# A delta-rule attention layer with a mixture of experts: later scatter waits, small scalings on ScalarE, padding a group ahead, a three-engine final sum

## The chip, the cores and the metric

The kernel runs on one core of one Trainium2 chip. The time is that of one execution on the device, in microseconds (us); a run gives one such time. The engines are TensorE (PE, its weight loads PEld), VectorE (DVE), ScalarE (ACT), GpSimd (POOL) and SyncE (SP, which here only issues DMAs). A q behind an engine's name (SPq, DVEq) is its instruction queue. Numbers such as L1143 are lines of the kernel before; the changed kernel's lines lie some 10 to 50 further down.

## The reference

The input is 2 x 2048 tokens of 128 features in float32. Two blocks follow, each on the layer-normed input and added to it.

```
x = x + attention(layernorm(x))
x = x + experts(layernorm(x))
```

The attention is a gated delta rule with 8 heads of 128 x 128 state. Projections give q, k and v, each run through a causal convolution of four taps; two more give the gates beta and alpha.

```
S = S * alpha_t ;  kv = k_t S ;  S = S + outer(k_t, (v_t - kv) * beta_t) ;  o_t = q_t S      (token by token)
out = (o / rms(o) * norm_w * silu(z)) @ out_w.T
```

The experts: a router picks the best 2 of 8 experts for each token, with softmax weights over these two; each expert computes `relu(x W1 + b1) W2 + b2` with 512 hidden features, and the two results are summed with their weights.

## The kernel before

**Chunks and groups.** The delta rule is computed in chunks of 128 tokens. With decays, key products and the inverse of a triangular matrix a chunk becomes matrix products, and only the state S goes from chunk to chunk. A group is two chunks (c = 0, 1), sixteen groups in all, and the eight heads are worked on in two halves (u = 0, 1). `stages(g, a, par)` finishes group g while it prepares group a = g + 1, on each engine in the same order, which is the long string `ORDER` (L248): a word such as `scale.0` is the step `scale` for chunk 0. Each engine walks through `ORDER` and issues what is its own; all else is done by semaphores. Groups 1 to 14 run in a hardware loop of two groups a turn (L643 for GpSimd, and the same on the others), so every second group begins with a turn of the loop. An engine executes its instructions in order: a wait holds everything behind it.

**Steps of a group that matter here.** `taps`, `first` and `last` are the convolution of one of sixteen weight tiles: ScalarE multiplies two taps (L749), VectorE adds two (L1111, L1114), GpSimd adds the halves (L625). `diag` (L617, GpSimd) and `scan` (L1122, VectorE) build the decays; `ka` and `aq` (L608) scale keys and queries by them, `sp` (L637) scales the state. `kk` is the product of the keys (TensorE), `nm` masks it. `scale` (L1143, L1144, VectorE) takes the decays of the chunk's end, 128 x 8 elements, for ScalarE's `kd` (L758) and for GpSimd's `sp`. `inv` are 22 parts of the triangular inversion on VectorE (L1006 to L1028). `sq` (L808, ScalarE) sums squares of the output, and `rms` (L1046 to L1056, with L229 to L236) is a chain of small VectorE steps to one over the root; `gn` (L817) scales by it, `gt` transposes, `out` projects, `x2` (L1190) adds the residual, which SP has loaded (`xl`, L483) and stores again (`xs`, L489).

**Routing.** Each finished group g is routed during the next one (`route`): `sm` and `s2` its layer norm on ScalarE, `nr` the normalised rows on GpSimd (L581, L584), `xt`, `lg` the router's logits, `rk` the ranks (L1057), `pf` and `ps` the places in the experts' regions (L1085), and `sc` four indirect DMAs on GpSimd (L597) that scatter the rows into the DRAM tensor `rows_in`, at the place that is next in their expert's region. `sw` at the end of `ORDER` (L588) waits for these four scatters before GpSimd's next group. `counts` holds where each expert's rows end.

**Between the two blocks.** The last group is routed after the loop. Then VectorE makes ready the experts' second bias `b2` as two float16 rows (L1229, L1230), copies the ends of the regions (L1235) and works out the table of the 39 tiles of 256 rows (L1236 to L1264): expert, first row, limit. SP writes 256 rows of zeros behind each expert's last row (L520 to L523, nine DMAs), so that a tile never reads rows that weren't written, and then gathers the tiles (L532). VectorE goes on with the first bias for all tiles (L1268, L1270) and the softmax weights of the two experts of each token (L1276 to L1285, with one exponential on ScalarE, L848).

**The expert tiles.** For tile t: gather, transpose (L1630), split into a high and a low float16 half (L853, L1295), `up` (twelve products, L1643), bias and relu (L860 and L1302), split again (L867, L1310), `down` (L1649: two products of one row each with `b2`, high and low, L1657, and twelve with W2 in each half), scaling (L1315), and two indirect DMAs that scatter 128 result rows each into `rows_out` (L655). Four buffers: VectorE's part of tile t (`low`, L1288) waits until the scatters of tile t - 4 have landed.

**The end.** SP loads `rows_out` in four pieces (L539), VectorE adds them to the residual with the tokens' weights, 64 operations of 128 x 128 (L1333), and SP stores each piece when it is done (L543).

## Time and profile before

| what | us |
|---|---|
| median of three runs | 1516.26 (1508.14 to 1516.53) |
| the profiled execution | 1505.35 |
| its span in the profile | 1503.5 |
| granted TensorE clock, mean | 0.92 of full speed |
| busy: PE, DVE, ACT, POOL | 1225.6, 1202.2, 810.1, 709.4 |
| groups of the delta rule | 186 to 1280, about 71 and 76 in turn |
| last routing, tables, padding | 1280 to 1312 |
| 39 expert tiles | 1313 to 1476 |
| load, final sum, store | 1476 to 1503.5 |
| gather of a tile, 130 KB, issue to landing | 2.2 |
| DMA rate from 1482 to 1488, all engines busy | 422 GB/s |

No engine is busy all the time, so the kernel is held by chains that pass from engine to engine. The rows further down have the start in us from the beginning of the span, the duration in us, the engine, the line, the operation, output and inputs with their shapes; in brackets how long the engine idled before and what ended that. A row with x2 or x8 sums that many operations. Operations on one engine overlap a little, so a start can lie before the end of the one before. In the rows of the chain of waits, "issue" is time in which the engine waited for nothing that the profile shows.

### The profile page before, as it was taken

To read this page: it belongs to the slowest core of one execution; us is meant where nothing else is said; L and a number is where in the kernel's file an instruction comes from. 1 tells how busy PE (TensorE), PEld (TensorE's weight loads), DVE (VectorE), ACT (ScalarE), POOL (GpSimd) and SP (SyncE) were. 2 spreads that over 40 slices of the span, in tenths; PEclk is the share of its full clock that TensorE was granted. 3 is DMA by queue.
4 is the path that set the end of the run, shared out by engine and by line. 5 is a ranking of instruction groups with operands and counts; after the bars stand their busy time and mean duration, and the time that the engine had idled before them with its cause. 6 is when DMAs were issued, how large, how long until landed. Compare 5 with 4: busy or idle time off the path is not lost.

```text
span 1503.5 us, 36893 instructions
## 1 busy us (share of the span) xinstructions
PE 1225.6 (82%) x12056; PEld 984.6 (65%) x12056; DVE 1202.2 (80%) x2660; ACT 810.1 (54%) x2401; POOL 709.4 (47%) x598
## 2 busy tenths in 40 slices
PE   0456988988898889898979897989798987299991
PEld 0334867766787677676767676768676866277771
DVE  6778898887888788969896988798878874677775
ACT  1243566564656566555656564656465656165550
POOL 4043554636373638272727282728273741244451
PEclk9987999999998999999989998899899999599996
DMA  6021221212131313120303131203121232422214
GB/s 193 0 85 36 59 65 36 75 33 75 34 79 33 76 31 91 33 75 24 99 19 85 24 89 34 74 20 89 41 68 41 67 90 52 122 63 66 64 52 169
DMA packets 164878, 96.29 MB, mean 64 GB/s; under 512 B 115622, under 2 KB 150060, under 8 KB 163778
## 3 DMA queue, kind: packets, MB, share of 16 engines
q1 hardware_dynamic: 126594, 81.05, 19.5%
q10 hardware_dynamic: 33536, 4.20, 1.8%
q0 software_dynamic: 4544, 8.47, 1.7%
q8 instruction: 110, 1.80, 0.5%
q14 instruction: 94, 0.77, 0.2%
HBM read 71.17 MB, written 23.41 MB: 63 GB/s over the span
## 4 chain that ended last, share of the span: by engine, by line
PE 29%; DVE 26%; issue 20%; ACT 8%; DMA 7%; POOL 6%; SPq 2%; DVEq 1%; POOLq 0%; ACTq 0%
PE kx L1499 5%; DVE blkT L1028 4%; DVE Y_sb L1024 4%; DMA rows_out<-rhs,e_dst 3%; DMA rows_in<-rowbuf,dest 2%; DVE area L1114 2%; PE rc L1566 2%; POOL kq L625 2%; PE rc L1557 2%; POOL rows_out L655 2%; PE kx L1593 2%; POOL rows_in L597 1%; PE ob L1600 1%; ACT area L758 1%; POOL kq L608 1%
## 5 line engine op out<-in xcount | busy, mean ns | idle before, releaser
L625 POOL TENSOR_TENSOR kq<-tapA,area 128x256 f32<-128x256 f32 x256 | 203.0, 805 | 292.0 <-DVE area L1114 291.0
L1111 DVE SCALAR_TENSOR_TENSOR tapA<-pj,taps,tapA 128x256 f32<-128x256 f32 x256 | 121.9, 476 | 85.5 <-ACT tapA L749 83.3
L749 ACT ACTIVATE area<-pj,taps 128x256 f32<-128x256 f32 x256 | 120.8, 472 | 125.0 <-PE pj L1513 119.0
L1024 DVE TENSOR_TENSOR Y_sb<-blkT,blkN 128x4 f32<-128x4 f32 (+18 forms) x304 | 161.7, 532 | 10.4
L608 POOL TENSOR_TENSOR kq<-kq,area 128x1024 f32<-128x1024 f32 x64 | 152.0, 2376 | 3.3 <-DMA rows_in<-rowbuf,dest 3.3
L597 POOL DMA_INDIRECT rows_in<-rowbuf,dest x64 | 67.8, 1059 | 179.8 <-DVE dest L1100 154.0
L1028 DVE TENSOR_REDUCE blkT<-Y_sb 128x2 f32<-128x4 f32 (+18 forms) x304 | 142.4, 469 | 4.7
L1499 PE MATMUL kx<-kq 128*128 128x128 f32 x1024 | 137.7, 284 | 9.9 <-ACT GTs L822 5.1
L1499 PEld LDWEIGHTS kx<-kq 128*128 128x128 f32 x1024 | 125.2, 196 | 19.2 <-issue 11.2
L655 POOL DMA_INDIRECT rows_out<-rhs,e_dst x78 | 79.3, 1016 | 94.6 <-DVE e_dst L1292 60.2
L617 POOL TENSOR_TENSOR decay<-ident,beta 128x1024 f32<-128x1024 f32 x32 | 78.6, 2456 | 93.8 <-DMA rows_in<-rowbuf,dest 46.9
L1548 PE MATMUL rc<-w_hi,xn_hi 128*128 128x512 f16 x256 | 102.6, 401 | 24.4 <-issue 24.4
L1114 DVE SCALAR_TENSOR_TENSOR area<-pj,taps,area 128x256 f32<-128x256 f32 x256 | 121.2, 473 | 0.0
L749 ACT ACTIVATE tapA<-pj,taps 128x256 f32<-128x256 f32 x256 | 120.9, 472 | 0.0
L1549 PE MATMUL rc<-w_lo,xn_hi 128*128 128x512 f16 x256 | 102.2, 399 | 0.0
L1550 PE MATMUL rc<-w_hi,xn_lo 128*128 128x512 f16 x256 | 101.7, 397 | 0.0
L1585 PE MATMUL ob<-S,kq 128*128 128x128 f32 x512 | 100.1, 277 | 0.0
L758 ACT ACTIVATE area<-kx,kd_scale 128x128 f32<-128x128 f32 x256 | 73.2, 371 | 48.2 <-DVE a_end L1144 39.1
L1586 PE MATMUL ob<-Us,area 128*128 128x128 f32 x512 | 99.0, 275 | 0.0
L1593 PE MATMUL kx<-ident,Gs 128*128 128x128 f32 x256 | 46.9, 327 | 62.6 <-ACT Gs L817 42.7
L637 POOL TENSOR_TENSOR S<-S,a_end 128x1024 f32<-128x1024 f32 x32 | 90.6, 2832 | 11.3 <-PE ob L1586 11.3
L808 ACT ACTIVATE area<-ob 128x128 f32<-128x128 f32 x256 | 67.4, 278 | 45.8 <-PE ob L1586 45.8
(305 smaller groups left out, 3659.6 us busy)
## 6 DMA issues: line engine op xcount, KB each, us to landing
area<-scr_alpha SPq DMA_DIRECT2D x32, 512.0 KB, 3.9
area<-scr_acum SPq DMA_DIRECT2D x32, 512.0 KB, 3.9
blkN<-scr_n SPq DMA_DIRECT2D x32, 256.0 KB, 3.8
area<-rows_in SPq DMA_DIRECT2D x39, 130.0 KB, 2.2
scr_n<-area SPq DMA_DIRECT2D x128, 32.0 KB, 1.6
area<-rows_out SPq DMA_DIRECT2D x4, 1024.0 KB, 8.0
kq<-in_x SPq DMA_DIRECT2D x4, 512.0 KB, 6.1
area<-in_conv_w SPq DMA_DIRECT2D x1, 2048.0 KB, 12.3
```

What stands on the lines that cost most here:

```text
L608: nc.gpsimd.tensor_tensor(t, t, acum_b[:, c, :, :], ALU.mult).then_inc(done, 1)
L625: nc.gpsimd.tensor_tensor(dst[:, n % H, :], tapA[:, n % RING, :], tapB[:, n % RING, :], ALU.add).then_inc(conv_done, 1)
L655: nc.gpsimd.indirect_dma_start(rows_out, bass.IndirectOffsetOnAxis(ap=e_dst[:, t % 4, b:b + 1], axis=0), y_rows[:, t % 4, b, :], None, bou ...
L749: ins = nc.scalar.activation(dst[:, n % RING, :], pj[n % 2][:, k:k + GT], ACT.Copy, scale=taps[:, t, k:k + 1])
L1024: ins = nc.vector.tensor_tensor(p4, bc(blkT[:, r0:, j:].rearrange("p r (o m) -> p r o m", o=1), [128, nr, w, wd]), bc(blkN[:, j:j + w, j:] ...
L1028: ins = nc.vector.tensor_reduce(blkT[:, r0:, j:j + w], p4, AX.X, ALU.add, negate=True)
L1111: nc.vector.scalar_tensor_tensor(out=tapA[:, n % RING, :], in0=pj[n % 2][:, 0:GT], scalar=taps[:, order[n], 0:1], in1=tapA[:, n % RING, :] ...
L1114: nc.vector.scalar_tensor_tensor(out=tapB[:, n % RING, :], in0=pj[n % 2][:, 2:2 + GT], scalar=taps[:, order[n], 2:3], in1=tapB[:, n % RING ...
L1499: ins = mm(o, lhs[:, hh, cs], rhs_[:, hh, cs], start=True, stop=True)
L1548: mm(rc[u][:, :], hi, wv_hi[:, k, w], start=(k == 0), stop=False)
L1549: mm(rc[u][:, :], hi, wv_lo[:, k, w], start=False, stop=False)
L1550: mm(rc[u][:, :], lo, wv_hi[:, k, w], start=False, stop=False)
```

## The change

- `sw` leaves `ORDER`. GpSimd waits for the scatters of a group in `nr` of the next routing, before it overwrites the rows. For that it has groups 1 and 2 outside its loop too, which makes one turn fewer.
- The step `scale` moves from VectorE to ScalarE, as two activations.
- The padding: `pads()` on SP stands in the last `stages`, ahead of `sc` (so behind `al`, `ac` and `xl.0` and ahead of `xs.0`, `xl.1` and `xs.1`). It loads `b2` twice, then waits for the ends of the regions as they are before the last routed group, which VectorE copies after the last `ps` in `stages`, and copies 512 rows of zeros for each expert, from a zeroed part of `rows_in` that SP wrote at the start. GpSimd's last `sc` waits for all of them.
- `b2` in two rows, high and low, under a product with two rows of ones: one product where there were two. VectorE prepares it ahead of the last group's `rms`.
- The bias table in two parts, for 8 tiles before the first tile and 31 after the second; the weights in ten steps behind the tiles 4, 6, ... 22, the exponential on ScalarE in tile 16.
- Final sum: ScalarE scales the first expert's rows in place, VectorE adds the second's with their weights, GpSimd adds ScalarE's rows to them for three pieces, VectorE for the last.

```diff
@@ ORDER @@
-            at.1.1 x2.1 ti xs.1 sw
+            at.1.1 x2.1 ti xs.1
@@ sync @@
+            zero = R.rearrange("p g h c -> p (g h c)")[:, 0:4 * ROW].rearrange("p (b n) -> p b n", b=4)
+            sp.wait_ge(s_zero, 1)
+            sp.dma_start(rows_in[SPARE:SPARE + 2 * TT, :].rearrange("(b p) n -> p b n", p=128), zero).then_inc(padded, 16)
+            sp.wait_ge(padded, 16)
+            def pads():
+                sp.wait_ge(rdiag, chunks(NG - 1, 1))
+                for c in range(GC):
+                    sp.wait_ge(R_ready[c], rounds(NG - 1))
+                for k in range(2):
+                    sp.dma_start(b2_raw[k:k + 1], b2.rearrange("(o e) d -> o e d", o=1)).then_inc(f_b2, 16)
+                sp.wait_ge(ends_ready, 1)
+                for e in range(NE):
+                    at = sp.value_load(tab_end[0:1, e:e + 1], min_val=0, max_val=SPARE - 2 * TT)
+                    sp.dma_start(rows_in[ds(at, 2 * TT), :], rows_in[SPARE:SPARE + 2 * TT, :]).then_inc(padded, 16)
...
                 for step, *arg in STEPS:
+                    if step == "sc" and isinstance(g, int) and g == NG - 1:
+                        pads()
...
-            sp.wait_ge(ends_ready, 1)
-            sp.dma_start(rows_in[SPARE:SPARE + TT, :].rearrange("(b p) n -> p b n", p=128), e_rows[:, 3]).then_inc(padded, 16)
-            for e in range(NE):
-                at = sp.value_load(tab_end[0:1, e:e + 1], min_val=0, max_val=SPARE - TT)
-                sp.dma_start(rows_in[ds(at, TT), :].rearrange("(b p) n -> p b n", p=128), e_rows[:, 3]).then_inc(padded, 16)
@@ gpsimd @@
                 if step == "nr":
+                    if not isinstance(r, int) or r:
+                        pool.wait_ge(scattered, r * (2 * GC * 16))
+                        pool.sem_inc(sends, 1)
...
-                elif step == "sw":
-                    pool.wait_ge(scattered, r * (2 * GC * 16) + 2 * GC * 16)
-                    pool.sem_inc(sends, 1)
                 elif step == "sc":
+                    if isinstance(r, int) and r == NG - 1:
+                        pool.wait_ge(padded, 16 * NE + 16)
...
-            with pool.Fori(0, (NG - 2) // 2) as i:
-                stages(2 * i + 1, 2 * i + 2, 0)
-                stages(2 * i + 2, 2 * i + 3, 1)
+            stages(1, 2, 0)
+            stages(2, 3, 1)
+            with pool.Fori(0, (NG - 4) // 2) as i:
+                stages(2 * i + 3, 2 * i + 4, 0)
+                stages(2 * i + 4, 2 * i + 5, 1)
...
+            for q in range(PIECES - 1):
+                pool.wait_ge(c_first, q + 1)
+                pool.wait_ge(c_second, q + 1)
+                rows_q = slice(PC * q, PC * q + PC)
+                nc.gpsimd.tensor_tensor(x_sb[:, rows_q, :], x_sb[:, rows_q, :], y_parts[q][:, :, 0, :], ALU.add).then_inc(c_done, 1)
@@ scalar (the same step leaves vector, L1135 to L1145) @@
+                    elif step == "scale":
+                        c, = arg
+                        if g is not None:
+                            act.wait_ge(sp_ready, chunks(g, c))
+                        act.wait_ge(acum_in[c], a * 16 + 16)
+                        act.wait_ge(decay_done, chunks(a, c))
+                        end = keep[:, ds(a, 1)] if c == GC - 1 else 1.0
+                        nc.scalar.activation(kd_scale[:, c, :], decay[:, c, :, C - 1], ACT.Copy, scale=end)
+                        nc.scalar.activation(a_end[:, c, :], acum_b[:, c, :, C - 1], ACT.Copy,
+                                             scale=end).then_inc(scale_ready, 1)
...
+                if t == 16:
+                    act.wait_ge(weight_step, 7)
+                    nc.scalar.activation(w_b, w_d, ACT.Exp).then_inc(exp_done, 1)
+            act.wait_ge(weights_ready, 1)
+            for q in range(PIECES):
+                act.wait_ge(y_in[q], 16)
+                for j in range(PC):
+                    c = q * PC + j
+                    ins = nc.scalar.activation(y_parts[q][:, j, 0, :], y_parts[q][:, j, 0, :], ACT.Copy, scale=w_a[:, c:c + 1])
+                ins.then_inc(c_first, 1)
@@ vector @@
+                        if isinstance(r, int) and r == NG - 2:
+                            dve.wait_ge(place_taken, routed(r))
+                            nc.vector.tensor_copy(tab_end, counts[:, :]).then_inc(ends_ready, 1)
...
+            dve.wait_ge(f_b2, 32)
+            chain(nc.vector.tensor_scalar(b2_hi, b2_raw, WSCALE, None, ALU.mult), t_step, steps)
+            chain(nc.vector.scalar_tensor_tensor(out=b2_both, in0=b2_raw, scalar=WSCALE, in1=b2_hi, op0=ALU.mult,
+                                                 op1=ALU.subtract), t_step, steps)
+            nc.vector.tensor_copy(b2_both[0:1], b2_hi[0:1]).then_inc(b2_ready, 1)
+            for p in range(2):
+                rms(NG, NG - 1, p)
...
                 results(t)
+                if t == 1:
+                    biases(SOON, NTILE)
+                elif t >= 4 and t % 2 == 0:
+                    weigh(t // 2 - 2)
...
             for q in range(PIECES):
                 dve.wait_ge(y_in[q], 16)
+                for j in range(PC):
+                    c = q * PC + j
+                    ins = nc.vector.scalar_tensor_tensor(out=x_sb[:, c, :], in0=y_parts[q][:, j, 1, :], scalar=w_b[:, c:c + 1],
+                                                         in1=x_sb[:, c, :], op0=ALU.mult, op1=ALU.add)
+                ins.then_inc(c_second, 1)
+            dve.wait_ge(c_second, PIECES)
+            dve.wait_ge(c_first, PIECES)
+            last = slice(PC * PIECES - PC, PC * PIECES)
+            nc.vector.tensor_tensor(x_sb[:, last, :], x_sb[:, last, :], y_parts[PIECES - 1][:, :, 0, :], ALU.add).then_inc(c_last, 1)
@@ tensor @@
-                    for k, t_ in enumerate((b2_hi, b2_lo)):
-                        mm(o, ones[0:1, :], t_[0:1, ds(e, 1), :].rearrange("p o n -> p (o n)"), start=(k == 0), stop=False)
+                    mm(o, ones[0:2, :], b2_both[:, ds(e, 1), :].rearrange("p o n -> p (o n)"), start=True, stop=False)
```

## Rows read from the trace of the kernel before

**Rows 1.** The chain of waits, summed by line, 186 to 1262 and 1330 to 1466 us.
```profile
by line: issue 22.9%; PE kx L1499 5.8%; DVE blkT L1028 5.1%; DVE Y_sb L1024 3.8%; DMA rows_in<-rowbuf,dest 3.3%; PE rc L1566 2.7%; POOL kq L625 2.6%; DVE area L1114 2.5%; PE rc L1557 2.4%; POOL rows_in L597 2.0%; ACT area L758 1.9%; PE kx L
...
by line: DMA rows_out<-rhs,e_dst 34.2%; issue 18.7%; POOL rows_out L655 14.2%; DVE area L1302 10.1%; ACT area L867 7.5%; DVE area L1310 7.2%; DVE rhs L1315 3.6%; DVE e_dst L1292 1.9%; DVE Us L1295 1.9%; POOLq L655 0.7%; DVEq L1291 0.2%; POO
```

**Rows 2.** VectorE in order of time, in three groups of the loop.
```profile
746.01 1.98 DVE L1143 TENSOR_SCALAR kd_scale<-decay 128x8 f32<-128x8 f32 x1
...
747.91 1.94 DVE L1144 TENSOR_SCALAR a_end<-area 128x8 f32<-128x8 f32 x1
...
756.81 0.76 DVE L1024 TENSOR_TENSOR Y_sb<-blkT,blkN 128x100 f32<-128x100 f32 x1
...
757.90 0.31 DVE L1024 TENSOR_TENSOR Y_sb<-blkT,blkN 128x144 f32<-128x144 f32 x1
...
764.42 0.16 DVE L1046 TENSOR_SCALAR rs<-stat 128x2 f32<-128x2 f32 x1
...
1206.86 0.15 DVE L1046 TENSOR_SCALAR rs<-stat 128x2 f32<-128x2 f32 x1
```

**Rows 3.** GpSimd in order of time, in the loop and at the last routing.
```profile
745.60 2.36 POOL L608 TENSOR_TENSOR kq<-kq,area 128x1024 f32<-128x1024 f32 x1
...
747.92 1.90 POOL L637 TENSOR_TENSOR S<-S,a_end 128x1024 f32<-128x1024 f32 x1
...
756.73 0.72 POOL L625 TENSOR_TENSOR kq<-tapA,area 128x256 f32<-128x256 f32 x1 [4.40 <-DVE area L1114]
...
797.25 1.50 POOL L625 TENSOR_TENSOR kq<-tapA,area 128x256 f32<-128x256 f32 x2 [6.33 <-DVE area L1114]
...
1296.69 1.84 POOL L597 DMA_INDIRECT rows_in<-rowbuf,dest  x1 [6.04 <-DVE dest L1100]
```

**Rows 4.** ScalarE in order of time, in three groups of the loop.
```profile
762.75 0.22 ACT L808 ACTIVATION_READ_ACCUMULATOR area<-ob 128x1 f32 x1
...
767.31 2.45 ACT L817 ACTIVATE Gs<-Gs,rs 128x128 f32<-128x128 f32 x8
...
878.41 0.47 ACT L749 ACTIVATE area<-pj,taps 128x256 f32<-128x256 f32 x1 [0.75 <-POOL kq L625]
...
1206.24 0.22 ACT L808 ACTIVATION_READ_ACCUMULATOR area<-ob 128x1 f32 x1
```

**Rows 5.** Waits, 186 to 1280 us: total us, times, longest.
```profile
POOL decay L617 <- DMA rows_in<-rowbuf,dest: 46.9, 13, 5.1
```

**Rows 6.** SP's DMA issues in order of time, at the last routing.
```profile
1281.11 0.37 SPq L483 DMA_DIRECT2D xres<-in_x  x1
...
1299.59 8.36 SPq L523 DMA_DIRECT2D rows_in<-area  x8
...
1310.47 6.16 SPq L532 DMA_DIRECT2D area<-rows_in  x6
```

**Rows 7.** The chain of waits in order of time: start, us, what.
```profile
1156.83 3.84 DMA rows_in<-rowbuf,dest
```

**Rows 8.** DMA queues (packets, MB, share) and issues (times, KB, us to landing).
```profile
q1 hardware_dynamic: 126594, 81.05, 19.5%
...
xres<-in_x SPq DMA_DIRECT2D x32, 64.0 KB, 3.3
```

**Rows 9.** VectorE in order of time, from the last routing to the end.
```profile
1284.72 0.29 DVE L1190 TENSOR_TENSOR xres<-ob,xres 128x128 f32<-128x128 f32 x1 [2.96 <-PE ob L1600]
...
1296.41 1.21 DVE L1230 SCALAR_TENSOR_TENSOR Y_sb<-T,blkT 1x1024 f16<-1x1024 f32 x1
...
1305.09 2.28 DVE L1268 TENSOR_TENSOR area<-Gs,GTs 128x1248 f32<-128x1248 f32 x1
...
1307.41 1.45 DVE L1270 TENSOR_REDUCE Gs<-area 128x156 f32<-128x1248 f32 x1
...
1328.00 0.16 DVE L1292 TENSOR_TENSOR e_dst<-area,Gs 128x2 uint32<-128x2 int32 x1 [1.44 <-DMA rows_out<-rhs,e_dst]
...
1482.51 17.39 DVE L1333 SCALAR_TENSOR_TENSOR kq<-area,Gs,kq 128x128 f32<-128x128 f32 x64 [9.76 <-DMA area<-rows_out]
```

More of the change, by code:

```diff
@@ L176, in preln_delta_moe_kernel @@
         scr_t = nc.dram_tensor("scr_t", (GC * NB * H, BLK, BLK), F32, kind="Internal").ap()
[L177 removed]
+        rows_in = nc.dram_tensor("rows_in", (SPARE + 2 * TT, ROW), F32, kind="Internal").ap()
         rows_out = nc.dram_tensor("rows_out", (2 * TOKENS, D), F32, kind="Internal").ap()
@@ L510, in _ @@
             sp.dma_start(b1_sb[:, :, :], b1.rearrange("e (f p) -> p e f", p=128)).then_inc(f_small, 16)
-            sp.wait_ge(rdiag, chunks(NG - 1, 1))
-            for c in range(GC):
-                sp.wait_ge(R_ready[c], rounds(NG - 1))
-            sp.dma_start(b2_raw[0:1], b2.rearrange("(o e) d -> o e d", o=1)).then_inc(f_small, 16)
             for c in range(GC):
@@ L1134, in prepare @@
                             invert(k, a)
-                    elif step == "scale":
-                        c, = arg
-                        if g is not None:
-                            dve.wait_ge(sp_ready, chunks(g, c))
-                        dve.wait_ge(acum_in[c], a * 16 + 16)
-                        dve.wait_ge(decay_done, chunks(a, c))
-                        end = keep[:, ds(a, 1)] if c == GC - 1 else 1.0
-                        nc.vector.tensor_scalar(kd_scale[:, c, :], decay[:, c, :, C - 1], end, None, ALU.mult)
-                        nc.vector.tensor_scalar(a_end[:, c, :], acum_b[:, c, :, C - 1], end, None,
-                                                ALU.mult).then_inc(scale_ready, 1)
                     elif step == "at":
@@ L1212, in _ @@
                 split_low(k)
-            for p in range(2):
-                rms(NG, NG - 1, p)
-            rank(NG - 1)
-            destinations(NG - 1)
             steps = [0]
@@ L1239, in _ @@
             chain(nc.vector.tensor_copy(t_n, t_int), t_step, steps)
-            chain(nc.vector.memset(t_zero, 0.0), t_step, steps)
             chain(nc.vector.tensor_tensor_scan(t_cum, t_n, t_zero, 0.0, ALU.add, ALU.add), t_step, steps)
```

95 lines of the change are left out of this document (48 added, 47 removed).

## The prediction

> **What bounds the kernel now.** I read the chain of waits first, summed by line for two stretches. Between 186 and 1262 us (fourteen groups of two chunks) no engine owns the chain: TensorE products, VectorE's inversion (L1024, L1028) and GpSimd's additions (L625) take turns. In the expert tiles (1330 to 1466 us) the scatter of the results and its issue on GpSimd hold half of it, and no TensorE line is among the leaders [rows 1]. So a step pays only where it shortens the piece that ends last, and I then read, engine by engine, the rows around each edit.
>
> Two rows stand out. The small scaling of chunk 0 (L1143, 128x8) took 1.98 us on VectorE, and its neighbour L1144 1.94 us, where such operations otherwise take 0.16 to 0.23 [rows 2]. Each ended when a GpSimd operation ended: L608 ran to 747.96 and L637 from 747.92 to 749.82 [rows 3]. A VectorE product of two SBUF operands shows the same: 128x100 took 0.76 us while L625 ran, the larger 128x144 just after it 0.31 [rows 2, 3]. VectorE and GpSimd therefore block one another for whole operations; ScalarE rows show nothing of the kind.
>
> **The small scalings on ScalarE.** Fourteen groups have this pair in the loop's stretch; in all of them L1143 waits some 1.98 us, in six also L1144. The freed VectorE time, 2 or 3.7 us, isn't the gain. The next barrier on VectorE is the first step of the rms chain (L1046), which needs ScalarE's squares (L808). In the group at 764 us the squares ended at 762.97 and L1046 began at 764.42: 1.45 us late. At 1206 us it was 1206.46 and 1206.86: 0.40 late [rows 2, 4]. Six groups are of the first kind, eight of the second. About 0.03 us stays as latency, so 6 x 1.42 + 8 x 0.37 = 11.5 us. The squares themselves come out of a TensorE stretch without gaps, so they don't move. Inside the rms chain the second pair (chunk 1) also goes: some 0.27 us in each of fourteen, 3.8. Behind the chain everything waits for it: ScalarE's eight scalings of G start at 767.31, right after [rows 4]. Sum: 15.3 us. On ScalarE the pair, at some 0.25 us each, lies where it idled before the second squares and before the keys' scaling, cost 0. GpSimd's long operations will meet the inversion's first operations instead, up to 1.9 us later than they could start. In the six groups that leaves more than 1.42; in the eight it can eat the 0.37. Bounds: 12.3 and 15.3.
>
> **Scatters awaited later.** At the end of a group GpSimd waits for its four scatters: 46.9 us in thirteen groups, 3.6 each, before L617 [rows 5]. That is not the gain either. The group before each turn of the loop has the wait covered: GpSimd later idles 6.33 us for VectorE anyway (at 797.25) [rows 3]. In the other seven GpSimd runs from L617 at 865.2 without a break until ScalarE and TensorE wait for its L625 (0.75 us at 878.41) [rows 3, 4]. Released 3.2 us earlier it still can't begin its first addition before VectorE delivers at 867.6, and VectorE's scan, which excludes additions too, still needs its turn. I step that through to 877.1 in place of 878.3, and ScalarE, full until then, gives back some 0.3: 1.0 us in seven groups, 7.0. Bounds 0 (GpSimd's time wasn't the end) and 1.3 x 7 = 9.1. The wait now stands before the next group's rows are written, some 60 us later, cost 0. GpSimd's two more unrolled groups move no turn of the loop relative to the other engines.
>
> **Padding a group ahead.** Before: the last group's first scatter issues at 1296.69, the nine paddings are issued from 1298.2 to 1308, and the first gather at 1310.47 waited for the last of them [rows 3, 6]. After, only the scatters bind: the fourth issue comes 4.2 us after the first and has landed 3.84 us after that [rows 7], 8.0 in place of 13.8: 5.8 gained. The table of tiles is ready before that. Against it stand two things. First, SP's order: the eight paddings now stand ahead of the store of chunk 0 and of the load of the last residual chunk (L483, issued at 1281.11 [rows 6], 3.3 us to landing [rows 8]). They wait for the counts at 1277.4 and take 8.36 us for eight [rows 6], so L483 goes out at 1286.3 and lands at 1289.6, and VectorE's last residual sum, at 1284.72 now [rows 9], comes 4.9 us later. Everything of the last routing hangs on that sum. Second, the bias work (0.67, 1.21 [rows 9], a copy of one row, together 2.4) moves from behind the routing to ahead of its rms chain, so it delays the scatter where it had delayed only the table. Net 4.9 + 2.4 - 5.8 = +1.5 us. A padding is now a copy of 512 rows from DRAM to DRAM, which the trace lacks. Lower bound: no delay of L483, net -3.4. Upper bound: the SP queue spent 19.5% of 16 x 1503.5 us on 126,594 packets [rows 8], 37 ns each; 4096 rows on 16 engines are 9.5 us, and 19 if reading and writing add up, which puts the sum 14 us late: +10.6. I take the issue's price, since 9.5 fits beside 8.4. The zeros at the start cost SP some 3 us, where the first scan has that much room.
>
> **One bias product.** Two TensorE products of a tile go (some 0.15 us). TensorE isn't on the tiles' chain [rows 1]: 0. Without that cover it would be 39 x 0.15 = 5.9 us.
>
> **Bias tables and weights between tiles.** The weights (some 4 us) and 31 of 39 tiles of the bias table leave the stretch before the first tile, where the gather now ends last: 0 gained beyond the above. The bias table cost 2.28 + 1.45 us; its later part, 31/39, is 3.0 us on VectorE after the second tile, where VectorE then idles 1.44 [rows 9]: +1.5. The ten weight steps (0.2 to 0.45 each) fall behind a tile's results, and VectorE idles some 1.8 us in every second tile for a scatter: 0, at worst 4. The exponential in ScalarE's tile 16 waits for VectorE: +0.3.
>
> **Final sum on three engines.** Now VectorE takes 17.39 us for 64 operations, 0.272 each [rows 9]. After: VectorE 32 of them, 8.7, one addition of 128x1024, GpSimd three of these at 2.36 (L608's size) [rows 3], ScalarE 32 scalings at 0.31, 9.8 [rows 4], all hidden. VectorE's operations have two SBUF operands and GpSimd's additions too, so by the rows above they exclude one another: 8.7 + 7.1 + 1.9 (1024/1248 of the bias product's 2.28) = 17.7, or +0.3. Were they side by side, ScalarE would end last: 9.8 + 1.9 = 11.7, a gain of 5.7. The Trainium skill says the first: in "SBUF — State Buffer", section "Who interferes with whom", a VectorE instruction with two SBUF inputs contends with a GpSimd instruction that reads SBUF, and whoever issues first blocks the other for the whole instruction. This case's trace agrees, with 0.76 against 0.31 us.
>
> **Sum.** -15.3 - 7.0 + 1.5 + 1.5 + 0.3 + 0.3 = -18.7 us. The profiled execution took 1505.35 us (span 1503.5), so 1486.6 for one like it. The median of the runs shown is 1516.26, 10.9 above; I carry the difference over: 1497.6.
>
> **Rivals.**
> - The waits only move (0.20). The cast and the products at the start of the inversion meet L608 and L637 in the scalings' place, and GpSimd's earlier start is given back to ScalarE. For it: GpSimd holds its long operations back to back there. Against: the six groups have more to give than a second block takes. -6 to -12 us, 1504 to 1510, within 1%.
> - The paddings delay the last residual chunk by a copy's full price (0.09): transition +10.6 in place of +1.5, 1507.
> - More overlaps than I allow (0.12): the final sum side by side and no delay of L483, -5.7 - 0.3 and -4.9: -29.6, 1487.
> - Slower (0.07): a padding isn't spread over the DMA engines. At the end all 16 together move 422 GB/s (table of the profile, ahead); one alone then moves 26 GB/s, 266 KB take 10 us and eight 81, from 1277.4 to 1358. The last scatter waits for them by the new condition, and starts at 1358 in place of some 1304: +54 - 18.7 = +35, 1552. It decides from about 3.3 us for a padding on: below, they end before that scatter. Against it: the copies are given as 512 rows of 520 bytes, and the gathers of such rows, 130 KB each, land in 2.2 us (same table).
>
> The Trainium skill speaks against that last rival: "DMA: Bandwidth & Descriptors", section "Why a DMA increments its semaphore by 16 and not by 1", has a copy spread over the largest number of engines up to 16 that divides its slowest dimension, and 16 divides 512. No row of this trace shows a copy between DRAM tensors.
>
> **Numbers.** About 1% (15 us) is what a measurement of this kernel can tell from no change. My own forecast has 0.50 and is faster by 1.2%; with the third rival, faster 0.62. The first two are within 1%: 0.29. Slower 0.09, the fourth rival and 0.02 for what I don't see. The bounds of all terms give -34 and, without the fourth rival, +8; with runs of before spreading over 8 us I take 1481 to 1512.
>
> **What would show it.** L1143 and L1144 on ScalarE below 0.3 us; L1046 within 0.1 us of the squares' end in all groups; L1006 or L1011 stretched when it meets L608 or L637; no idle time before L617; in every second group L625 earlier by 1 us; L483 of the last group landing near 1289 on the scale of before, and the sum L1190 waiting for it; the gather right behind the last scatter; a gap of 1.5 us at the third tile; VectorE's and GpSimd's operations alternating in the final sum. I am wrong if the inversion loses more to GpSimd than the scalings did, if a padding takes over 3 us, or if the final sum ends before 1495 on that scale.

## The result

The changed kernel takes 1492.53 us in the median of four runs (1489.5 to 1502.42), the kernel before 1516.39 in the runs beside them. The ratio over all runs is 0.986, with a 95% interval of 0.983 to 0.990, or 21 us less (the medians differ by 24). I had forecast 1497.6 and a range of 1481 to 1512: 5 us too slow, on the right side. Several terms behind that number were far off, in opposite directions, so that the sum came out close is partly luck, and the parts matter more.

**The profile after.** Its profiled execution has a span of 1487.7 us, that of before 1503.5. First lines of the page of the changed kernel (busy time, mean ns, idle time and what ended it; for the DMA: times, KB, us to landing):

```profile
span 1487.7 us, 36679 instructions
...
L632 POOL TENSOR_TENSOR decay<-ident,beta 128x1024 f32<-128x1024 f32 x32 | 92.8, 2900 | 46.9 <-DVE w_lo L1020 38.6
...
rows_in<-rows_in SPq DMA_DIRECT2D x8, 260.0 KB, 3.9
```

GpSimd's wait for the scatters before L632 (L617 before [rows 5]) is gone: of the 46.9 us of idle time that are left there, 38.6 is one wait at the start. A padding of 260 KB lands 3.9 us after its issue. That is past the 3 us that I had named as a sign of being wrong, but nothing like the 10 us of my fourth rival: the eight are issued 1.3 us apart, land side by side, and are over long before the last scatters.

**In the loop.** VectorE, ScalarE and GpSimd of the changed kernel in order of time, in the eighth group, which answers to [rows 2, 3, 4] (start, us):

```profile
735.68 2.08 DVE L1051 TENSOR_TENSOR Y_sb<-blkN 128x512 f32<-128x512 f32 x1
...
750.03 0.17 DVE L1086 TENSOR_SCALAR rs<-stat 128x2 f32<-128x2 f32 x1
```
```profile
749.78 0.22 ACT L840 ACTIVATION_READ_ACCUMULATOR area<-ob 128x1 f32 x1
...
751.20 0.32 ACT L790 ACTIVATE kd_scale<-decay,keep 128x8 f32<-128x8 f32 x1
751.40 0.32 ACT L791 ACTIVATE a_end<-area,keep 128x8 f32<-128x8 f32 x1
...
752.83 2.44 ACT L849 ACTIVATE Gs<-Gs,rs 128x128 f32<-128x128 f32 x8
```
```profile
735.12 2.10 POOL L652 TENSOR_TENSOR S<-S,a_end 128x1024 f32<-128x1024 f32 x1
```

The squares end at 750.00 and the rms chain (L1086) starts at 750.03. Before, it started 1.45 us late at 764.42. The scalings of chunk 1 cost ScalarE 0.32 us each, those of chunk 0 0.23. The inversion's first product (L1051) ends at 737.76, 0.54 after GpSimd's L652 does, and takes 2.08 us, where it took 0.92 in the kernel before. In six of the sixteen groups it takes 2.08 and in a seventh 1.94, in the others 0.7 to 1.4: the block has moved there in part, as expected, and it no longer delays the chain.

**Where the time went.** Stage by stage, from the starts in the traces. The loop is from the first to the fifteenth rms chain, fourteen groups; a tile starts with VectorE's small step for its scatter (L1292 in [rows 9]).

| stage | before, first profile | before, second profile | after |
|---|---|---|---|
| start of the first rms chain | 252.95 | 252.89 | 249.58 |
| loop | 1013.37 | 1026.46 | 992.59 |
| fifteenth rms chain to first tile | 46.46 | 45.70 | 49.30 |
| first to last tile | 151.87 | 151.74 | 155.20 |
| last tile to the landing of the first piece | 17.86 | 18.12 | 17.96 |
| first piece to the end | 20.99 | 20.99 | 23.07 |
| span | 1503.5 | 1515.9 | 1487.7 |

The second profile of before comes from the first experiment below. It shows that the one under the prediction had a short loop. The gain is in the loop, but for 3.4 us ahead of it, and that start varies from 249.6 to 254.8 us among the kernels with the same start as the changed one. The stages behind the loop lost 8 to 9 us, where I had counted with 3.6.

**The clock.** Windows over whole groups, from rms chain to rms chain: the stretch and its length; the busy time of TensorE, its weight loads, VectorE, ScalarE and GpSimd, each with its number of instructions; the granted clock of TensorE as a share of full speed; DMA share, GB/s. The kernel before, first profile, then its second profile, then the changed kernel:

```profile
841.11:912.24 71.13, 63.99 (x644) 52.32 (x644) 62.87 (x132) 43.43 (x135) 38.06 (x31) 0.95 0.22 57
912.24:991.08 78.84, 68.56 (x644) 54.41 (x644) 61.79 (x133) 43.41 (x135) 38.19 (x31) 0.89 0.19 52
```
```profile
769.42:848.19 78.77, 68.53 (x644) 54.40 (x644) 61.78 (x132) 43.46 (x135) 38.17 (x31) 0.89 0.20 52
...
919.99:996.13 76.14, 65.53 (x636) 52.39 (x636) 60.58 (x132) 42.38 (x132) 38.61 (x31) 0.91 0.21 54
```
```profile
750.03:825.37 75.34, 65.73 (x646) 52.53 (x644) 59.70 (x128) 43.49 (x139) 39.09 (x31) 0.93 0.22 55
825.37:893.41 68.04, 62.92 (x646) 51.87 (x644) 58.99 (x127) 43.49 (x139) 39.06 (x31) 0.97 0.24 59
```

The same products (644 or 646 in the rows) take 68.5 us of TensorE's time at a clock of 0.89 and 65.7 at 0.93, and the group is 78.8 us long or 75.3. After the change ten of the fourteen groups are alike: 68.0 at 0.97 or 75.3 at 0.93. Before, they went from 70.1 to 71.9 and from 74.9 to 78.8. In all groups of these two kernels the clock falls 4 to 7 us behind the start of the rms chain, and in most a second time, in nearly every second group some 25 us behind it. The first 8.89 us from the chain's start in the ninth group, the kernel before and then the changed one:

```profile
841.11:850.00 8.89, 4.29 (x23) 3.60 (x23) 8.18 (x25) 5.38 (x18) 1.79 (x3) 0.72 0.01 2
```
```profile
825.37:834.26 8.89, 5.85 (x38) 4.64 (x36) 8.27 (x23) 7.37 (x25) 1.76 (x3) 0.87 0.00 1
```

Here TensorE runs out of work until VectorE and ScalarE have normalised the outputs. It was busy for 4.29 us of that stretch before and for 5.85 after, and its granted clock was 0.72 (more than half of the stretch at the lower level, 1.2 of 2.4 GHz) against 0.87. So a stall of VectorE at that point can be paid for twice: once as the stall, once in products at half the clock behind it. How much of the gain is the second part isn't settled; the kernel with the scalings alone, below, bounds it.

### The profile page after: what moved, and what is told of

It reads as the page before. It is cut to its first block, busy times and chain, and to the rows that moved or that the text cites. A ratio compares the mean times of both kernels' runs of the same rounds, so it can differ in the third digit from the quotient of the medians.

```text
span 1487.7 us, 36679 instructions
## 1 busy us (share of the span) xinstructions
PE 1205.9 (81%) x11978; PEld 972.7 (65%) x11978; DVE 1163.0 (78%) x2567; ACT 823.2 (55%) x2497; POOL 731.9 (49%) x601
## 4 chain that ended last, share of the span: by engine, by line
PE 44%; issue 13%; ACT 13%; DVE 12%; POOL 9%; DMA 6%; SPq 1%; POOLq 1%; DVEq 0%; ACTq 0%
PE kx L1548 5%; PE rc L1615 4%; PE ob L1634 4%; PE ob L1635 4%; DMA rows_out<-rhs,e_dst 3%; PE rc L1606 3%; PE rc L1623 3%; ACT area L780 2%; ACT Gs L849 2%; POOL rows_in L612 2%; PE rc L1597 2%; PE rc L1598 2%; PE rc L1599 2%; POOL kq L623 2%; ACT tapA L771 2%
## 5 line engine op out<-in xcount | busy, mean ns | idle before, releaser
L640 POOL TENSOR_TENSOR kq<-tapA,area 128x256 f32<-128x256 f32 x256 | 196.3, 776 | 308.5 <-DVE area L1154 307.5
L623 POOL TENSOR_TENSOR kq<-kq,area 128x1024 f32<-128x1024 f32 x64 | 152.3, 2382 | 0.0
L632 POOL TENSOR_TENSOR decay<-ident,beta 128x1024 f32<-128x1024 f32 x32 | 92.8, 2900 | 46.9 <-DVE w_lo L1020 38.6
L652 POOL TENSOR_TENSOR S<-S,a_end 128x1024 f32<-128x1024 f32 x32 | 93.2, 2912 | 16.1 <-PE ob L1635 16.1
L840 ACT ACTIVATE area<-ob 128x128 f32<-128x128 f32 x256 | 67.2, 277 | 42.8 <-PE ob L1635 42.8
L1560 PE MATMUL pj<-xn_hi,w_hi 128*128 (+1 forms) x256 | 73.3, 286 | 14.9 <-DVE area L1154 6.9
```

The lines of the kernel that those rows point to most:

```text
L623: nc.gpsimd.tensor_tensor(t, t, acum_b[:, c, :, :], ALU.mult).then_inc(done, 1)
L640: nc.gpsimd.tensor_tensor(dst[:, n % H, :], tapA[:, n % RING, :], tapB[:, n % RING, :], ALU.add).then_inc(conv_done, 1)
```

## The experiments

Each ratio is to the kernel before in runs on the same chip, with its 95% interval. The stages are those of the table above, each from one profile. The changed kernel has 0.986 (0.983 to 0.990).

| kernel | ratio | loop | to first tile | tiles | first piece to end |
|---|---|---|---|---|---|
| before, again | | 1026.5 | 45.7 | 151.7 | 21.0 |
| scalings alone | 0.984 (0.980 to 0.987) | 1003.5 | 45.6 | 150.8 | 21.0 |
| later scatter wait alone | 0.999 (0.997 to 1.001) | 1016.9 | 46.4 | 150.9 | 21.0 |
| changed, scalings back | 1.002 (0.999 to 1.005) | 1021.8 | 49.9 | 152.3 | 23.0 |
| changed | 0.986 (0.983 to 0.990) | 992.6 | 49.3 | 155.2 | 23.1 |
| changed, paddings later | 0.981 (0.978 to 0.985) | 991.6 | 43.2 | 160.2 | 23.0 |
| changed, sum of before | 0.985 (0.982 to 0.988) | 990.4 | 49.0 | 154.0 | 21.5 |
| changed, sum on two engines | 0.982 (0.979 to 0.985) | 990.6 | 48.9 | 155.0 | 17.4 |
| changed, one bias wait | 0.987 (0.984 to 0.990) | 990.3 | 49.1 | 155.0 | 23.0 |
| changed, whole bias table first | 0.987 (0.982 to 0.992) | 994.2 | 50.4 | 156.1 | 23.1 |
| changed, two bias products | 0.984 (0.980 to 0.989) | 997.0 | 49.7 | 159.0 | 23.1 |
| both gains | 0.982 (0.978 to 0.986) | 990.7 | 42.3 | 162.3 | 17.5 |
| both gains, second bias later | 0.982 (0.977 to 0.987) | 1000.8 | 42.8 | 152.3 | 17.4 |

**The kernel before, profiled again.**

> The kernel before, unchanged, profiled a second time. The profiled execution of before that the prediction is summed against took 1505.35 us, 11 us under the median of its runs, that of the changed kernel 3 us under its own. If the kernel before varies by how deep TensorE's granted clock falls behind the rms chain (the clock hypothesis), this profile is longer than 1503.5 by groups with a mean clock of 0.90 and less where the first had 0.93 to 0.95, at 3 to 5 us a group. Rival, the difference lies elsewhere (at the start or in the tiles): the groups take 70 to 72 and 75 to 77 us again, and their sum from the first to the fifteenth rms chain is within 3 us of 1013.4.

It took 1517.74 us, close to the median of before. The loop was 13.1 us longer than in the first profile, nothing else by more than 0.8. In ten of its fourteen groups the rms chain came 1.45 us late, in the first profile in six. That is 4 us of stalls more. TensorE was busy for 916.2 us of the loop in place of 905.2, with the same 8909 products, at a mean granted clock of 0.92 in place of 0.93. So the clock hypothesis holds in the main: even groups at 0.89 take 78.8 us in both profiles, the three at 0.93 in the first took 74.9 to 76.9. So the 11 us between the first profile and the median, which the prediction carried over as a constant, lay in the stage that the change shortens.

**The scalings alone.**

```
-  dve: kd_scale, a_end = nc.vector.tensor_scalar(..., end, None, ALU.mult)
+  act: kd_scale, a_end = nc.scalar.activation(..., ACT.Copy, scale=end)
```

> The kernel before with one part of the change: the two small scalings of a chunk (128x8) on ScalarE in place of VectorE. My theory: 15.3 us less (bounds 12.3 and 15.3), 0.990 of before, all of it between the first and the fifteenth group; the rms chain begins within 0.1 us of the end of the squares in every group. Rival, the waits only move to the inversion's first operations: 0 to 6 us less, 0.996 to 1.000. Rival, the two parts of the loop need each other (both had to be taken away before GpSimd's additions come earlier): under 12 us less here, under 5 in the kernel with the scatter wait moved alone, and their sum well under the 21 us that the changed kernel gained between those two groups.

0.984, which is 24.6 us (19 to 30) and no less than all the change brought. My bound of 15.3 is refuted, and so are both rivals as they stood: what waits took the scalings' place (the inversion's first product took 1.85 to 2.09 us in five groups, before 0.92) didn't delay the chain, and the gain didn't need the other part. In twelve of fourteen groups the chain starts 0.03 us behind the squares.

The profile also bounds the clock's share. Against the second profile of before the loop is 23.0 us shorter and TensorE was busy for 909.0 us in place of 916.2; against the first it is 9.9 us shorter, though TensorE was busy for 3.8 us more. So most of what this part gave in the profiles is TensorE's idle time, and some 7 us at most are products that ran at a better clock.

**The later scatter wait alone.**

```
   if step == "nr":
+      if r: pool.wait_ge(scattered, r * 64)
...
-  elif step == "sw": pool.wait_ge(scattered, r * 64 + 64)
```

> The kernel before with one part of the change: GpSimd awaits the four scatters of a group ahead of the next group's rows, not at the group's end, and has two more groups unrolled. My theory: 7.0 us less (bounds 0 and 9.1), 0.995 of before, in the seven groups that aren't followed by a turn of the loop, 1.0 us each, and nothing in the others. Rival, GpSimd's time was not the end: 0 us. Rival, the freed wait is worth most of its 3.6 us in seven groups: 15 to 25 us less.

0.999, or 2 us less (from 5 less to 1 more). That lies within my bounds, and the 7 that I took lie outside the interval. The third case (15 to 25 us) is out. The trace shows where the rest went. Three of the seven groups it is meant for take 69.2 us at a clock of 0.95, where such groups took 70.1 to 71.4 before, so GpSimd's earlier start does bring 1 to 2 us. But others gave it back, one most of all (the window over it):

```profile
840.23:914.92 74.69, 68.46 (x644) 56.03 (x644) 61.81 (x132) 43.24 (x135) 38.18 (x31) 0.89 0.21 54
```

This group has the same 644 products and takes 5 us more. What is missing is clock, but not behind a gap (two stretches in its middle):

```profile
862.00:872.50 10.50, 10.37 (x209) 6.61 (x207) 9.18 (x17) 6.24 (x16) 9.05 (x7) 1.00 0.52 110
872.50:882.70 10.20, 10.20 (x69) 8.82 (x67) 6.49 (x13) 6.25 (x15) 6.24 (x7) 0.50 0.29 112
```

TensorE was busy for 10.37 of 10.50 us at full clock and then stood at half of it for 10.20 us, busy all the time. The ninth group of two other kernels shows the same: scalings alone (73.95 us at 0.86) and both gains with the second bias later (73.84 at 0.86). So neither the scatter wait nor a late chain makes it (in the kernel with the scalings alone the chain was 0.03 us behind the squares), and why the clock falls there stays open.

**The changed kernel with the scalings back on VectorE.**

> The changed kernel with the two small scalings back on VectorE. By the price of the scalings alone (24 us less in the runs, 10 to 12 in the profile), undoing them costs 18 to 25 us: a ratio of about 1.000 to before. By my prediction's term it costs 15.3: 0.995. Rival, the later wait for the scatters already makes GpSimd free, so that the scalings no longer meet it: under 8 us, 0.990.

1.002: undoing this one part costs 24 us, as its price alone said, and leaves nothing of the change. With both parts in, the loop took 990 to 1001 us in nine profiles; with the scalings alone 1003.5 in one; with the scatters alone or with neither, 1013 to 1026 in four. So in the runs the scatter wait brings nothing clear while the scalings stand. Once they are gone, the loop is 11 us shorter with it (1003.5 to 992.6), but 6 of these are the one slow ninth group, which a kernel with both parts has too (1000.8). At a clock of 0.97 to 0.98 the odd groups took 68.8 us with the scalings alone and 68.0 to 68.1 with both parts: 0.75 us a group, near the 1.0 that I had forecast, or some 5 us in seven groups. The runs don't resolve it: those with the scalings alone aren't slower than those of the changed kernel.

**The paddings behind the last residual load.**

```
-  if step == "sc" and g == NG - 1: pads()
+  if step == "xs" and arg[0] == GC - 1 and g == NG - 1: pads()
```

> The changed kernel with the eight paddings issued behind the load of the last residual chunk and the store of chunk 0, not ahead of them. Theory (what the paddings cost is their place in SyncE's order, not their transfer): the last residual sum comes some 18.4 us after the fifteenth rms chain begins, in place of 25.4, and the kernel is 5 to 7 us faster than the changed one, about 0.982 of before. Rival, the transfer is what counts: the copies, now under the last routing, hold up the last group's scatters, which wait for them, and 3 us or less are gained. The paddings would have to land later than 30 us after the fifteenth rms chain for that.

0.981, 8 us better than the changed kernel by the ratios, whose intervals overlap a little (0.983 to 0.990 and 0.978 to 0.985), so the gain is shown in the stage and not yet in the total. SP and VectorE of the changed kernel at the last routing, which answer to [rows 6, 9]:

```profile
1254.38 9.82 SPq L447 DMA_DIRECT2D rows_in<-rows_in  x8
...
1264.93 0.37 SPq L502 DMA_DIRECT2D xres<-in_x  x1
...
1289.20 0.39 SPq L542 DMA_DIRECT2D area<-rows_in  x1
```
```profile
1267.62 0.29 DVE L1219 TENSOR_TENSOR xres<-ob,xres 128x128 f32<-128x128 f32 x1 [10.26 <-DMA xres<-in_x]
...
1270.34 1.21 DVE L1257 SCALAR_TENSOR_TENSOR blkT<-T,Y_sb 2x1024 f16<-2x1024 f32 x1
...
1272.06 0.17 DVE L1086 TENSOR_SCALAR rs<-stat 128x2 f32<-128x2 f32 x1
```

VectorE idles 10.26 us, until a residual lands whose load stood behind eight issues, 9.82 us for all. The last residual sum starts 25.45 us after the fifteenth rms chain, before 18.40. SP of the experiment:

```profile
1261.21 0.37 SPq L502 DMA_DIRECT2D xres<-in_x  x1
...
1263.54 9.73 SPq L447 DMA_DIRECT2D rows_in<-rows_in  x8
...
1287.41 2.69 SPq L542 DMA_DIRECT2D area<-rows_in  x3
```

The load goes first, the sum follows 18.47 us after the chain, and the stretch to the first tile falls from 49.3 to 43.2. GpSimd's idle time ahead of the last scatters is 6.04 and 6.05 us, so the transfers delayed nothing here: it was the place in the queue.

**The final sum of before, and one on two engines.**

> The changed kernel with the final sum of before: VectorE's 64 scaled additions alone, no GpSimd and no ScalarE in it. Theory (VectorE and GpSimd block one another, and the pieces of the sum end bunched, so that their stores do too): from the landing of the first piece to the end of the span 21.0 us as before, in place of 23.1, so 2 us faster than the changed kernel. Rival, three engines do help: 0.7 to 6 us slower than the changed kernel.

21.5 us from the first piece to the end and a ratio of 0.985. In the profile three engines are 1.5 us slower than VectorE alone; in the runs the two can't be told apart. By the profile the rival, that three engines help, is out.

```
   # ScalarE as in the changed kernel: y0 = y0 * w_a;  GpSimd: nothing
   for q in range(4):
       x += y1 * w_b            # VectorE, eight operations
+      x += y0                  # VectorE, one of 128x1024
```

> The changed kernel with GpSimd out of the final sum: ScalarE scales one half, VectorE adds the other half and, in four additions of 128x1024, the first. By the prices in the traces VectorE needs 32 x 0.27 + 4 x 1.2 to 1.9 = 13.4 to 16.2 us and stores each quarter as it ends: from the landing of the first piece to the end of the span 17 to 20 us, against 23.1 with three engines and 21.0 to 21.6 with VectorE alone. 3 to 6 us faster than the changed kernel. Rival, ScalarE's scaling of the last piece or the stores set the end: no gain, 21 to 23 us.

17.4 us and 0.982. The sum of the changed kernel, GpSimd and VectorE, which answers to the last of [rows 9]:

```profile
1464.63 2.19 DVE L1380 SCALAR_TENSOR_TENSOR kq<-area,Gs,kq 128x128 f32<-128x128 f32 x8 [10.06 <-DMA area<-rows_out]
...
1467.11 2.46 POOL L679 TENSOR_TENSOR kq<-kq,area 128x1024 f32<-128x1024 f32 x1 [8.83 <-ACT area L915]
1467.28 2.44 DVE L1380 SCALAR_TENSOR_TENSOR kq<-area,Gs,kq 128x128 f32<-128x128 f32 x1
...
1471.44 6.25 POOL L679 TENSOR_TENSOR kq<-kq,area 128x1024 f32<-128x1024 f32 x1 [1.87 <-DVE kq L1380]
1471.74 3.75 DVE L1380 SCALAR_TENSOR_TENSOR kq<-area,Gs,kq 128x128 f32<-128x128 f32 x14
1475.53 3.25 DVE L1386 TENSOR_TENSOR kq<-kq,area 128x1024 f32<-128x1024 f32 x1
1477.65 3.32 POOL L679 TENSOR_TENSOR kq<-kq,area 128x1024 f32<-128x1024 f32 x1
1477.72 0.39 SPq L556 DMA_DIRECT2D out<-kq  x1
```

The same on two engines:

```profile
1469.26 2.18 DVE L1372 SCALAR_TENSOR_TENSOR kq<-area,Gs,kq 128x128 f32<-128x128 f32 x8
1471.47 1.23 DVE L1378 TENSOR_TENSOR kq<-kq,area 128x1024 f32<-128x1024 f32 x1
1472.61 2.18 DVE L1372 SCALAR_TENSOR_TENSOR kq<-area,Gs,kq 128x128 f32<-128x128 f32 x8
1474.83 1.22 DVE L1378 TENSOR_TENSOR kq<-kq,area 128x1024 f32<-128x1024 f32 x1
```

Without GpSimd beside it VectorE's addition of 128x1024 takes 1.23 us, with it 3.25. GpSimd's three take 2.46, 6.25 and 3.32 us. The rows show them taking turns. One scaled addition of VectorE, 0.35 us otherwise, is held for 2.44 until GpSimd's first addition is over. GpSimd's second is issued at 1471.44, but VectorE's scaled additions run on at their usual pace of 0.27 until 1475.49, and it ends 2.2 us after them, at 1477.69. VectorE's own addition, begun at 1475.53, ends 1.1 us after that, and GpSimd's last one 2.2 us later still. The Trainium skill ("SBUF — State Buffer", section "Who interferes with whom") has the two engines lock one shared pair of ports, so that one blocks the other for whole instructions; these rows agree.

**One wait for the bias table in place of one in each tile.**

```
-  wait_ge(bias_ready, 1 if t < SOON else 2)          # ScalarE and VectorE, all 39 tiles
+  if t in (0, SOON): wait_ge(bias_ready, 1 if t < SOON else 2)
```

> The changed kernel, in which ScalarE and VectorE wait for the bias table only ahead of the tiles 0 and 8, where the changed kernel repeats this wait in all 39 tiles. Tiles 24 to 38 took 55.8 us before and 58.2 after, though nothing else in them was changed. Theory, the repeated waits are instructions on the tiles' chain (some 0.1 us each on two engines): tiles 24 to 38 take 55.8 again, all tiles some 5 us less than after, ratio 0.983. Rival, the tiles vary with the landing of their scatters: no difference, 58 us with a spread of 1.5, ratio 0.986.

0.987 and 155.0 us for the tiles: no difference, and my theory falls. Its tiles 24 to 38 took 54.8 us, but tiles 4 to 24 took 83.4.

**The whole bias table before the first tile, and two bias products.**

> The changed kernel with the whole bias table made ahead of the first tile, as before; the weights stay between tiles. In the changed kernel VectorE idles 2.33 us for the first gather after the first part of the table (1.0 us); the whole takes 2.28 + 1.45, so the first tile starts 0.4 us later and tiles 0 to 4 take 15.2 us again in place of 16.7: 1 us faster than the changed kernel, a ratio of 0.986 as it has (my term of +1.5 for this part). Rival, the tiles' loss (38 tiles take 155 us in place of 151.5) all comes from this part: 3 to 4 us faster, tiles 4 to 24 and 24 to 38 shorter too.

The first four tiles are back at 15.3 us from 16.7, the stretch before them is 1.0 us longer, and the ratio stays. The rival (all of the tiles' loss comes from here) is out: the other tiles took 140.8 us, in the changed kernel 138.5.

```
-  mm(o, ones[0:2], b2_both[:, e], start=True)
+  for k, t_ in enumerate((b2_hi, b2_both)): mm(o, ones[0:1], t_[0:1, e], start=(k == 0))
```

> The changed kernel with the two bias products of before (two more TensorE products of 1x128 by 1x128 in each half of a tile, and no copy of the row). Theory, TensorE isn't on the tiles' chain: no difference, within 1 us, ratio 0.986. Rival, it is: 39 tiles x 0.15 = 5.9 us slower, 0.990.

0.984 with an interval of nearly a whole per cent: no cost is seen in the ratio. In its one profile the tiles took 159.0 us, against 152.3 to 162.3 in the seven profiles with the changed kernel's tiles, so a cost of a few us isn't excluded by it. One of its six runs took 3999.43 us and is left out of the ratio; nothing on record explains it.

**Both gains together, and the second bias later.**

> The changed kernel with both gains at once: the eight paddings behind the load of the last residual chunk, and the final sum on ScalarE and VectorE without GpSimd. Theory, they lie in different stretches and add up: 43.2 us from the fifteenth rms chain to the first tile in place of 49.3, and 17.4 us from the first piece to the end in place of 23.1, 12 us faster than the changed kernel, ratio 0.977. Rival, the tiles are slower behind the shorter transition (155 us in the changed kernel, 160 in the profile with the paddings moved): 6 to 7 us faster, 0.981.

The two stages add up in the profile (42.3 and 17.5 us), but its tiles took 162.3, and the ratio is 0.982, no better than that of either gain by itself. Of the two forecasts the second was the right one.

> As the one with both gains, and VectorE's work on the second bias (0.67, 1.21 and 0.41 us) moved from ahead of the last group's rms chain to behind the table of tiles, where VectorE idles 2.33 us for the first gather. Theory, it delays the last scatters where it stands: another 2.4 us less, 40.8 from the fifteenth rms chain to the first tile, ratio 0.975. Rival, the first tile is then late by the same work, or the table: 0 to 1 us less.

0.982 again. The last rms chain came 2.2 us sooner (20.5 us after the fifteenth, in place of 22.7), but the first tile 0.5 later. With the second bias out of the way the last group's scatters were ready sooner and met a new wait, GpSimd at the last routing (and, after it, SP's first gathers):

```profile
1281.58 1.03 POOL L609 DMA_INDIRECT rows_in<-rowbuf,dest  x1 [6.79 <-DMA rows_in<-rows_in]
...
1290.91 4.99 SPq L542 DMA_DIRECT2D area<-rows_in  x5
```

The scatters now wait for the paddings, which had been moved behind the load; that costs 0.75 us, since GpSimd idles 6.04 us for VectorE at this place in the changed kernel. The first gather comes 5.45 us after the last scatter's issue (1285.46), in the changed kernel 3.12 (1289.20 after 1286.08). SP had issued the load of the residual, 2 MB, at 1280.88, just ahead of the first scatter, in the changed kernel at 1269.62, 12.4 us ahead of it. In the two other kernels with the paddings moved it was issued 2.5 and 2.7 us ahead, and the gather came 4.14 and 3.46 us after the last scatter. That the load slows the scatters fits all four; it is argued, not tried. Both combined kernels beat the kernel before by some 1.8%. Their medians, 1491.0 and 1485.9, don't show that they beat the changed kernel with one gain alone.

## Why the prediction came out right, point by point

**Scalings, -15.3.** The mechanism was right, with rows about as forecast (0.23 and 0.32 us on ScalarE against 0.25, the chain 0.03 us behind the squares in all groups but the first, L1051 stretched to 2.08), but the size was wrong: 24.6 us alone, 24 when undone. The step that failed is "about 0.03 us stays as latency, so 6 x 1.42 + 8 x 0.37". It had two gaps. The profile at hand was one of the good ones: with the ten late groups of the second profile the same sum gives 10 x 1.42 + 4 x 0.37 + 3.8 = 19.5. And the sum had no term for TensorE's clock, though the page of before showed it below full speed and windows over the groups would have shown 0.89 to 0.95 in step with their lengths. What is left, 24.6 against 19.5, is within the interval (19 to 30), so that the clock makes it up is argued and not shown.

The Trainium skill ("TensorE: Matmul & The Clock Gate", section "HAM oscillation — how this bites in real kernels") says that gaps between bursts of products make the products after them run at the lower clock. The windows behind the chain agree, with 0.72 against 0.87. The slow ninth group doesn't fit it: there the clock fell behind 10.5 us in which TensorE was busy for 10.37. I hadn't weighed that rule.

**Scatters, -7.0.** Alone 2.1 us, with an interval that goes from 5.2 less to 0.9 more. The mechanism was right: undisturbed groups gained 1 to 2 us, and 0.75 at the same clock once the scalings were gone. The step that failed is to take "1.0 us in seven groups" as a sum that reaches the end: other groups were longer by as much, at a lower clock. The two terms came to 22.3 and the two parts to 21 in the loop of the first profile (1013.4 to 992.6) and 34 in that of the second. Their order of size was right only as a pair.

**Padding and last routing, +1.5.** Measured +2.8 and +3.6 (46.46 and 45.70 to 49.30). The order on SP was the cause, as forecast. The sizes: the residual sum came 7.05 us later, not 4.9, since the eight issues took 9.82 in place of 8.36 and began 12.2 us after the fifteenth rms chain, not 11.1. The upper bound, a copy's full price, had no counterpart. The second bias was 2.4 as forecast (0.67, 1.21, 0.41 and a memset). From the sixteenth rms chain to the first gather 23.74 became 17.14, a gain of 6.6 for which I had 5.8.

**One bias product, 0.** Within 4 us of that; see above.

**Bias tables +1.5, weights 0, exponential +0.3.** The table is confirmed (rows after the second tile of the changed kernel):

```profile
1305.14 1.93 DVE L1302 TENSOR_TENSOR area<-Gs,GTs 128x992 f32<-128x992 f32 x1
1307.11 1.19 DVE L1304 TENSOR_REDUCE Gs<-area 128x124 f32<-128x992 f32 x1
```

That is 3.0 us on VectorE, of which 1.5 shows. But the tiles as a whole are slower: 151.7 and 151.9 before and 150.8 to 150.9 in two kernels with their old order, against 152.3 to 162.3 in the ten profiles of the changed kernel and its variants, 156.1 in the mean. Tiles 24 to 38, in which nothing of the work is changed, took 55.1 to 57.6 us in four of the old order and 54.8 to 60.2 in ten of the new. Undoing the repeated waits, the table or the one product, one at a time, didn't bring it back. The weights between the tiles weren't tried by themselves, so my 0 for them isn't confirmed and the cause of some 3 us stays open, as does why profiles with a short way to the first tile had tiles of 160 and 162 us in two cases and 152 in the third.

**Final sum, +0.3.** Measured +2.1 to the end of the span. The exclusion was right and was even priced too high: the last addition ended 16.3 us after the first piece, not 17.7. The step that failed is that the sum alone was priced. Before, each quarter was done 4.3 us after the one before and its store ran beside the next; the last store ended 3.6 us after the last addition. Now the second and third quarters leave GpSimd at 1477.69 and 1480.97 and the fourth VectorE at 1478.78. SP stores them in their order, so the fourth waits behind the third, both are issued 0.4 us apart (1481.00 and 1481.41), and the span ends 6.7 us after the last addition.

**The base.** I carried the 11 us from the profile to the median over as a constant. It was 3 us after the change. The difference is which execution the profile caught, in a loop that goes on varying: the four runs of the changed kernel lie within 13 us, those of before within 16. So the constant was no property of the kernel, and that it did little harm is luck. Against the median the scalings gave some 9 us more than forecast, the stages behind the loop took some 5 more and the scatter wait by itself gave some 5 less; that they cancel brought the forecast to within 5 us. The range's upper end was tighter than my own bounds: +8 on the median of before would be 1524, not 1512.

**Rivals.** The waits did move, but nearly for free; the paddings' transfer, the fuller overlap of the sum and the slow copy did not happen. The slow copy would have needed 10 us on one DMA engine, by the prediction's estimate; it landed in 3.9. The Trainium skill ("DMA: Bandwidth & Descriptors", section "Why a DMA increments its semaphore by 16 and not by 1") spreads a copy of 512 rows over 16 engines, and the 3.9 us are in line with that.

## What to carry to other kernels

A stall at a point where TensorE has run dry can cost more than its length: read the granted clock over windows of the loop's own period, and take a second profile, before pricing a stall that comes and goes. Where a step issues DMAs, look at what stands behind it in that queue and at who waits for that; the transfers themselves were free here, the place was 6 us. Don't run VectorE beside long GpSimd operations on SBUF where the chain waits for it: not only additions of two operands were held here, but also L1143 with one, for 1.98 us. Count a store's queueing with the computation that feeds it.

## What the runs showed of the hardware that I had not expected

- The loop of one kernel took 1013 us in one profile and 1026 in another, in step with TensorE's granted clock: odd groups took 71.1 us at 0.95 and (scatter wait alone) 74.7 at 0.89, even ones 74.9 at 0.93 and 78.8 at 0.89, with the same 644 or so products.
- TensorE's clock fell to 0.50 for 10.2 us behind 10.5 us in which the engine was busy for 10.37, in the ninth group of three kernels.
- A copy between two DRAM tensors of 260 KB costs SP 1.23 us (9.82 / 8), of which the issue itself is 0.53 and the rest is reading its address into a register; one of 130 KB from SBUF cost 1.04 (8.36 / 8), with 0.37 for the issue. The larger one lands in 3.9 us.
- VectorE's addition of 128x1024 took 1.23 us beside an idle GpSimd and 3.25 beside a busy one; one of GpSimd's, issued amid VectorE's stream of small additions, took 6.25, where another took 2.46.
- The 39 tiles took from 152 to 162 us in eight profiles whose tiles do the same work, at a granted clock of 0.94 to 1.00 behind the first four.
